# Products of constants on TensorE in the two waits for returned expert rows

## The reference

```
x = x + L0_attn(norm(x))        # retention with decay, causal
x = x + L0_xattn(norm(x), ctx)  # one head over the context
x = x + L0_ffn(norm(x))         # 8 experts, the 2 best of each token, no capacity
x = x + L1_attn(norm(x))        # causal attention, 16 heads, rotated
x = x + L1_xattn(norm(x), ctx)  # 16 heads over the context
x = x + L1_ffn(norm(x))         # 8 experts, top 2 with a capacity, and a shared expert
```

## Time and profile before

| | |
|---|---|
| median of 3 runs | 1499.17 us (1488.19 to 1499.22) |
| profiled execution | 1501.88 us, of which span 1500.1 us |
| mean granted TensorE clock | 0.939 |
| PE busy | 1331.1 us (89%), 15723 instructions |
| DVE, ACT, POOL busy | 932.4 us, 833.2 us, 581.3 us |

### The profile page before, as it was taken

The page is one execution under the profiler, slowest core; times in us unless marked ns, Lnnn a source line. Parts: engine busy times, 40 slices in busy tenths (PEclk is TensorE's granted clock), DMA queues, the critical chain, the costliest instruction groups (busy, mean ns, idle before and its releaser), DMA issues. The chain is left out here.

```text
span 1500.1 us, 42118 instructions
## 1 busy us (share of the span) xinstructions
PE 1331.1 (89%) x15723; PEld 1002.1 (67%) x15723; DVE 932.4 (62%) x1638; ACT 833.2 (56%) x1366; POOL 581.3 (39%) x622
## 2 busy tenths in 40 slices
PE   7888999828997877899999999999999999987884
PEld 3544766527884553677777777777777777756774
DVE  3333555485652694677777777777777777628552
ACT  5554333334652474366666666666666666656671
POOL 2210000246751564443443344344344344232773
PEclk9959999958998997899999999999999999997998
DMA  3053999241103002955655755755755665513213
GB/s 87 22 138 92 253 256 235 75 135 37 43 23 99 2 2 71 195 124 139 157 121 132 164 119 126 164 125 121 164 131 122 156 136 121 113 44 92 63 36 92
DMA packets 72299, 169.87 MB, mean 113 GB/s; under 512 B 16430, under 2 KB 43832, under 8 KB 72208
## 3 DMA queue, kind: packets, MB, share of 16 engines
q1 hardware_dynamic: 64976, 149.48, 41.1%
q10 hardware_dynamic: 2688, 11.78, 2.8%
q0 software_dynamic: 4544, 7.36, 1.7%
HBM read 84.52 MB, written 9.47 MB: 63 GB/s over the span
## 5 line engine op out<-in xcount | busy, mean ns | idle before, releaser
L2203 DVE TENSOR_REDUCE hat_tops<-banks 128x1 f32<-128x500 f32 x672 | 439.3, 676 | 151.7 <-PE banks L1948 150.8
L2076 ACT ACTIVATE hat_pb<-banks 125x896 f32<-125x896 f32 x384 | 340.2, 916 | 220.3 <-PE banks L1967 215.4
L1948 PE MATMUL banks<-hat_kh,hat_qm 128*128 128x500 f32 x672 | 298.5, 463 | 4.5 <-DVE hat_tops L2203 3.3
L1967 PEld LDWEIGHTS banks<-hat_q,hat_k 128*125 128x125 f32 x1536 | 219.3, 188 | 73.2 <-ACT hat_pb L2076 31.8
L1967 PE MATMUL banks<-hat_q,hat_k 128*125 128x224 f32 x1536 | 250.2, 286 | 14.6 <-ACT hat_pb L2076 9.1
L2145 POOL CAST hat_kh<-hat_kf 128x500 fp32r<-128x500 f32 x96 | 58.6, 611 | 399.3 <-ACT hat_kf L2089 385.0
L1958 PE MATMUL banks<-hat_pb,hat_vs 125*27 125x168 f32 (+1 forms) x6144 | 166.9, 261 | 0.1
L1958 PEld LDWEIGHTS banks<-hat_pb,hat_vs 125*27 125x27 f32 (+1 forms) x6144 | 132.0, 98 | 44.0 <-issue 24.3
L1948 PEld LDWEIGHTS banks<-hat_kh,hat_qm 128*128 128x128 f32 x672 | 128.1, 192 | 44.0 <-DVE hat_tops L2203 29.5
L2151 POOL TENSOR_TENSOR hat_kl<-hat_kf,hat_kh 128x500 fp32r<-128x500 f32 x96 | 119.4, 1272 | 0.4 <-DMA hat_k<-hat_kh 0.4
L1978 PEld LDWEIGHTS banks<-w_HWvT,hat_ct 128*125 128x125 f32 x768 | 99.3, 190 | 5.3 <-ACT hat_vs L2083 0.5
(11 more groups left out here) (377 smaller groups left out, 2534.5 us busy)
## 6 DMA issues: line engine op xcount, KB each, us to landing
hat_k<-hat_kh SPq DMA_DIRECT2D x256, 187.5 KB, 4.7
hat_ct<-ctxT SPq DMA_DIRECT2D x32, 750.0 KB, 6.2
hat_k<-hat_kl SPq DMA_DIRECT2D x128, 187.5 KB, 4.5
ctx_cx<-ctx SPq DMA_DIRECT2D x32, 672.0 KB
ctx_cd<-ctxT ACTq DMA_DIRECT2D x15, 750.0 KB, 7.6
moe_raw<-Mw SPq DMA_DIRECT2D x18, 256.0 KB, 3.4
ctx_cx<-ctx SPq DMA_DIRECT2D x32, 78.0 KB
ffn_raw<-FWgT SPq DMA_DIRECT2D x8, 256.0 KB, 2.8
```

The source lines that it names most:

```text
L1948: peak_out.inc(nc.tensor.matmul(g.bank(PK + m % 2)[:, 0:SB], qm[u][:].rearrange("p h i -> p (h i)")[:, r * 128:r * 128 + 128], kh[u][:, c ...
L1967: mm = nc.tensor.matmul(g.bank(2 * (t % 2) + j // 2)[0:SW, (j % 2) * QW:(j % 2 + 1) * QW], k3[u][:, j, t * SW:(t + 1) * SW], q3[u][:, j, : ...
L2076: exped.inc(nc.scalar.activation(pb[t % 6][:].rearrange("p (n i) -> p n i", n=2), g.ps[0:SW, 2 * (t % 2):2 * (t % 2) + 2, 0:2 * QW], ACT.E ...
L2203: peaked.inc(v.tensor_reduce(tops[:, r, n:n + 1], g.bank(PK + m % 2)[:, 0:SB], AX_X, ALU.max))
```

## The change

Two waits and two calls of the helper are added on TensorE, one pair in each expert stage, after the last product of the experts and ahead of the wait for the first returned group.

```
@@ experts0, TensorE
                 pe.wait_ge(lots_made, 2)
                 pe.wait_ge(made, TILES)
+                pe.wait_ge(x_low, TILES)
+                keep_warm(g, 6, 19)
                 for i, (a, b) in enumerate(GROUPS):
                     pe.wait_ge(back_in[i], 32)
@@ experts1
     GROUPS = [(0, 4), (4, 8), (8, 12), (12, 14)]
+    WARM = 30
@@ experts1, TensorE
                 turn_out(E - 1)
                 pe.wait_ge(lots_made, 2)
+                pe.wait_ge(biased_out, E)
+                keep_warm(g, 0, WARM)
                 for i, (a, b) in enumerate(GROUPS):
                     pe.wait_ge(back_in[i], 32)
```

## The result

The kernel with the change takes 1511.69 us (median of 4 runs, 1509.52 to 1525.23) against 1497.46 us before (4 runs, 1488.19 to 1499.22): a ratio of 1.0107 with a 95% interval of 1.007 to 1.0145, so slower by some 16 us of 1497, between 10 and 22 (the two medians lie 14.2 us apart). The forecast was 1512 us. The profiled execution took 1512.07 us (span 1510.3 us, mean granted clock 0.946 where it was 0.939): the clock is higher and the kernel slower.

A forecast was written before the change was run, and what follows sets the result against it. It took the returning rows, not PE, to bound both layers' ends, with fillers overrunning the waits: 5.0 + 7.6 = +12.6 us, about 1512 us on the median of 1499.17; range 1498 to 1519, the forecast's own 1509 to 1517.

The forecast's parts named there:

- What bounds: At both layers' ends PE idles 8.10 and 13.26 us until returned rows land; each join then starts at half clock.
- The price of a product: Each added product is two instructions, 0.75 us; 19 last 14.25 us and 30 last 22.5, beyond waits of 8.1 and 13.3.
- First layer: End of the first expert layer: join starts 6.8 us later and is 1.75 us shorter, +5.0 us.
- term of 0.8 us for a cold start: First filler starts at half clock until about 450.3 us, costing 0.8 us; the ends are zero and 1.75.
- Second layer: End of the second expert layer: products at full clock, join 9.1 us later and 1.47 us shorter, +7.6 us.
- a fall worth up to 1.75 us: Second filler: should the clock fall once during its products, one half-clock spell costs up to 1.75 us more.
- Sum: Both expert layers together: +12.6 us, between +10.3 and +15.3; 0.84% of the time, chance 0.82.
- The signs of being wrong: A join still waiting for its transfer, half clock during the filler, or the gap between layers changing over 2 us.
- What the clock gives back: Both joins wholly at full clock save 1.75 and 1.47 us, together at most 3.2 us, 0.2% of the span.
- the products fit: Rival: both fillers end inside the waits, at 0.376 us a product; -3.2 us, 1496 on the median; chance 0.05.
- A later stage tipped into half clock: Rival: the shift puts the causal attention loops at half clock, up to +27 us, about 1539; chance 0.09.
- the low end of the forecast: +10.3 us: first filler at full clock, 0.8 less, and no half-clock spell at the next stage's start, 1.5 less.

The follow-up runs named there:

- first_only: The changed kernel without the second call: only the 19 products of the first expert layer; ratio 1.0025 to the kernel before.
- double: The changed kernel with 38 and 60 products in place of 19 and 30; ratio 1.034 to the kernel before.
- half_columns: The changed kernel with the same 19 and 30 products, each 224 columns wide in place of 448; ratio 1.0012 to the kernel before.
- fit: The changed kernel with 9 and 15 products in place of 19 and 30; ratio 0.9991 to the kernel before.
- bridged: The changed kernel with 10 and 16 products in the waits and one more ahead of each last step; ratio 1.0006 to the kernel before.
- waits_only: The changed kernel with both calls left out and the two added waits kept; 1497.65 us in one run.

## Why the prediction was right

**What bounds.** Right. The joins were released by transfers; with fillers that fit they are again, and with the change by PE.

**The price of a product.** This was the step that decides, and it held: 0.75 us, read from an existing call. 38 instructions filled 443.06 to 457.39 us, 14.33 us or 0.754 a product, at full clock (14.25 had been forecast). The spacing that the Trainium skill gives in "TensorE: Matmul & The Clock Gate", section "Back-to-back issue gap", 189 ns for 448 columns by an estimate, is not that of these products. The four passes of the Trainium skill's "FP8 and Floating Point Precision", section "TensorE Precision Notes", 747 ns by an estimate, agree with the 754 ns measured.

**First layer.** Forecast +5.0, measured +4.23: the join starts 14.39 us behind the last down product in place of 8.41 (+5.98), and from its start to the next stage's first product it is 10.11 us in place of 11.86 (-1.75). The forecast term of 0.8 us for a cold start was not paid, because in this execution the clock had not fallen ahead of the filler; in first_only it had, and the term was there with 0.81 us.

**Second layer.** Forecast +7.6, measured +9.35: the join starts 24.82 us behind the transposes in place of 14.00 (+10.82), saves 1.49 us, and the tail is unchanged. The term that was mis-sized is the clock: I took it as full, with a fall worth up to 1.75 us as the bound, and the fall came (0.50 from 1475.6 to 1479 us) and cost 1.5 us in the filler and 0.2 in the transposes. In double, without a fall, the join starts 45.68 us behind the transposes, close to the 45.6 us that 60 products of 0.75 us and 0.6 us of transposes make.

**Sum.** 13.6 us in the stretches, against 12.6 and bounds of 10.3 to 15.3; with the 2.2 us in between, 15.8. The forecast put the whole just under the 1% line, and the measured ratio is just above it, with both sides of the line in its interval. That the median of 1511.69 us lies within 0.5 us of the forecast is luck: the four runs are up to 15.7 us apart, and the errors of the two layers, -0.8 and +1.7 us, partly cancel.

**The signs of being wrong.** Two that the prediction had named showed, both small. The clock was at half for 3.4 us of the transposes and the second filler, and the stretch between the layers grew by 2.2 us, where a change of more than 2 was to count. Neither touches the price of a product or the order on PE, on which the forecast rests.

**What the clock gives back.** The 1.75 and 1.47 us of the forecast came (1.75 and 1.49) where all transfers had landed before the join began. Where the filler fits, only 1.5 and 0.9 us are left, because then the transfers of the later groups set the join's pace; in no run here was the bound of 3.2 us all to be had.

**The rivals.** That the products fit was the right point of decision: with products at half the price (half_columns) the loss vanishes. A later stage tipped into half clock came as well, but small: some 1.4 us, not 27. The stretch between the two measured ones is 1004.9 to 1005.8 us in the three profiles without a first filler, and 1005.4 to 1007.7 us in the six with one. Part of the difference lies in the loops of the causal attention. The products there that read the tile rot_kb (its rows before and after; the last two times are the first and the last start) are spread over 56.7 us in each of the three profiles, and over 58.0 to 58.4 us in each of the six:

```profile
L1734 PE MATMUL banks<-rot_kb,rot_part x256: 347/370/392, 503.2 to 559.9; 32*56 32x224 f32 x128
...
L1736 PE MATMUL banks<-rot_kb,rot_part x256: 347/370/508, 500.3 to 558.4; 32*56 32x224 f32 x128
```

All six have a spell at half clock early in these loops, with the change 0.50 from 509.6 to 513.0 us; the three hold 1.00 throughout. fit, half_columns and bridged have it too, though their first stretch is shorter than before, so it is not the delay that brings it. Why a filler ahead of the stage goes with it, no run shows.

At the start of the stage it was the other way round. The prediction wrote that the stage had kept full clock throughout, which the earlier trace rows contradict for its first products; with the change these lost their spell at half clock, as the low end of the forecast allowed (PE in order of time, answers to the earlier trace rows):

```profile
476.71 1.02 PE L1631 MATMUL banks<-xn,w_RwqT 128*128 128x448 f32 x2 [1.99 <-DVE xn L300]
477.56 0.92 PE L1632 MATMUL banks<-xn,w_RwqS 128*128 128x448 f32 x2
478.32 0.92 PE L1631 MATMUL banks<-xn,w_RwkT 128*128 128x448 f32 x2
```

With the change the two cancel: counted from the first product of line 259, the first product on rot_kb starts about 1.5 us earlier than before and the last about 0.1 us earlier. The 2.2 us arise behind the loops, where a spell at half clock is longer (0.51 from 564.1 to 581.4 us, before 0.51 from 566.3 to 580.1 us). Whether that spell belongs to the change or to chance stays open, as does what makes the unchanged work ahead of the first stretch end anywhere from 441.6 to 448.6 us in the nine profiles.

## What to carry to other kernels

Size a filler in time, from a row of the same product in the same kernel at both clock levels, and let it end before the awaited transfer lands; count a float32 product by its two instructions. Everything beyond the wait was paid in full here, while the gain is at most half of the time that the next work would have spent at half clock, and less if transfers set that work's pace. A filler can also go with a spell at half clock in a later stage, so the whole time decides and not the stretch alone. A mean clock that rises says nothing: here it rose from 0.939 to 0.946 as the kernel got slower.

## What the runs showed of the hardware that was not expected

The granted clock's rise is not as regular as the three rows of the kernel before had it (3.0 to 3.5 us after dense work began): in waits_only it took until about 1488.8 us, 6.1 us after the join began at 1482.64 us, with PE busy all the way. Nor does the same idling always end the same way. PE in order of time ahead of the last down products, with the change, in fit, and before:

```profile
440.09 0.38 PE L1412 MATMUL banks<-ffn_down_both,ffn_hh 128*128 x1 [0.48 <-DVE ffn_ow L1578]
442.09 0.38 PE L1412 MATMUL banks<-ffn_down_both,ffn_hh 128*128 x1 [0.87 <-DVE ffn_ow L1578]
...
442.94 0.38 PE L1412 MATMUL banks<-ffn_down_both,ffn_hh 128*128 x1 [0.33 <-DVE ffn_ow L1578]
444.94 0.38 PE L1412 MATMUL banks<-ffn_down_both,ffn_hh 128*128 x1 [0.87 <-DVE ffn_ow L1578]
...
444.93 0.38 PE L1412 MATMUL banks<-ffn_down_both,ffn_hh 128*128 x1 [0.33 <-DVE ffn_ow L1576]
```

With the change and in fit the clock stayed at 1.00 after these waits; in the kernel before, waits of 0.33 and 0.87 us, the same two as in fit, were followed by a fall at 446.9 us.
